# The vector engine's chained functions of an adaLN transformer kernel, divided at their joints and dealt among one another

## The reference

```python
mod = (silu(c) @ wmod).reshape(32, 6, 1, -1)          # sa, ca, ga, sb, cb, gb
ga = sign(ga) * max(|ga|, 0.25); gb the same
h = layernorm(x) * (1 + ca) + sa
x = x + ga * attention(h)        # rmsnorm, 16 heads of 64, causal softmax,
                                 # sigmoid gate per head, output projection
h = layernorm(x) * (1 + cb) + sb
x = x + gb * ffn(h)
# ffn: silu(h @ Wg + bg) * (h @ Wu + bu) @ Wd + bd, plus experts:
#   q = h @ Wq; sim with 64 keys for each of 4 heads and 2 halves
#   top 8 of each half, all sums of the two, the top 8 of those, softmax
#   sum over these 8 of 512 experts: silu(h . down[e]) * weight * up[e]
```

## Time and profile before

| | us |
|---|---|
| median of 3 runs | 1448.64 |
| lowest and highest | 1445.79, 1448.77 |
| span of the profiled execution | 1448.7 |
| PE busy | 1399.7 (97%) |
| DVE busy | 1289.4 (89%) |
| ACT busy | 1270.9 (88%) |
| POOL busy | 1052.9 (73%) |

### The profile page before, as it was taken

How to read it: one execution, slowest core, us unless ns; L and a number is a source line. 1 busy time by engine, 2 the same in 40 slices (tenths; PEclk the granted TensorE clock), 3 DMA queues, 4 the chain that set the end, 5 groups by cost and what they waited for, 6 DMA issues and landing times.

```text
span 1448.7 us, 39838 instructions
## 1 busy us (share of the span) xinstructions
PE 1399.7 (97%) x11491; PEld 1161.5 (80%) x11491; DVE 1289.4 (89%) x5345; ACT 1270.9 (88%) x4212; POOL 1052.9 (73%) x1221
## 2 busy tenths in 40 slices
PE   6899999999999999999999999999999999999998
PEld 4678788888788888788888788888788888788887
DVE  5589999999999999999999999999999999999977
ACT  6788988898988898988898988898988898988885
POOL 2048787778787777787777787787787777777760
PEclk9999999999999999999999999999999999999999
DMA  4000000000000000000000000000000000000000
GB/s 132 16 14 21 15 10 20 20 16 20 13 11 20 20 16 20 14 10 20 20 16 20 13 11 20 20 16 20 15 9 20 20 16 20 14 10 24 10 14 10
DMA packets 51041, 27.74 MB, mean 19 GB/s; under 512 B 10336, under 2 KB 50208, under 8 KB 51008
## 3 DMA queue, kind: packets, MB, share of 16 engines
q1 hardware_dynamic: 50768, 26.91, 7.1%
q10 hardware_dynamic: 240, 0.43, 0.1%
HBM read 23.02 MB, written 4.31 MB: 19 GB/s over the span
## 4 chain that ended last, share of the span: by engine, by line
PE 81%; ACT 14%; issue 3%; DVE 1%; DMA 0%; SPq 0%; POOL 0%; ACTq 0%; DVEq 0%; POOLq 0%
PE pW L1457 10%; PE pS L1527 9%; PE pW L1540 9%; PE pW L1568 8%; PE pW L1459 8%; PE pW L1458 8%; PE pS L1517 7%; PE pS L1513 6%; PE pW L1613 4%; PE pW L1610 4%; ACT pT L652 4%; ACT pS L660 4%; PE pW L1544 3%; PE pW L1601 2%; ACT h L750 2%
## 5 line engine op out<-in xcount | busy, mean ns | idle before, releaser
L660 ACT ACTIVATE pS<-pS,nmx 128x128 f32<-128x128 f32 (+1 forms) x1024 | 389.4, 433 | 33.2 <-DVE nmx L1085 33.2
L1085 DVE CUSTOM_DVE_ANT_0 pS<-pS,mask 128x128 f32<-128x128 f32 (+1 forms) x1024 | 331.8, 390 | 27.2 <-PE pS L1517 22.7
L504 POOL TENSOR_TENSOR fexp<-fexp,fsum 128x512 f32<-128x512 f32 x240 | 299.9, 1284 | 76.6 <-DVE fexp L1214 76.6
L652 ACT COPY pT<-pS 128x768 f32<-128x768 f32 x256 | 216.1, 844 | 42.2 <-PE pS L1527 40.4
L495 POOL TENSOR_TENSOR fsum<-ex 128x512 f32<-128x512 f32 x248 | 250.6, 1047 | 0.0
L1527 PE MATMUL pS<-ident,p_sb 128*128 128x128 f32 x1536 | 216.3, 277 | 6.1 <-DVE p_sb L1105 4.2
L1105 DVE TENSOR_TENSOR p_sb<-pS,coef 128x256 f32<-128x256 f32 (+2 forms) x512 | 210.5, 453 | 8.9
L1527 PEld LDWEIGHTS pS<-ident,p_sb 128*128 128x128 f32 x1536 | 173.7, 141 | 37.3 <-issue 18.9
L660 ACT ACTIVATION_READ_ACCUMULATOR pS<-pS,nmx 128x1 f32 x1024 | 193.7, 189 | 0.0
L642 ACT COPY qk<-pW 128x512 f32<-128x512 f32 x256 | 162.2, 634 | 4.6 <-PE pW L1459 1.1
L1540 PE MATMUL pW<-pT,v 128*64 128x256 f32 x1024 | 165.9, 402 | 0.3 <-ACT pT L652 0.2
(11 more groups left out here) (211 smaller groups left out, 3696.1 us busy)
## 6 DMA issues: line engine op xcount, KB each, us to landing
x_in<-in_L_attn_tokens SPq DMA_DIRECT2D x32, 128.0 KB, 2.1
x_res<-in_L_attn_tokens SPq DMA_DIRECT2D x32, 128.0 KB, 3.0
modB<-mods_dram SPq DMA_DIRECT2D x32, 128.0 KB, 2.9
modA<-mods_dram SPq DMA_DIRECT2D x31, 128.0 KB, 3.1
out<-yo SPq DMA_DIRECT2D x31, 128.0 KB, 1.9
modC<-mods_dram SPq DMA_DIRECT2D x32, 64.0 KB, 3.2
fsum<-in_L_attn_Wkv SPq DMA_DIRECT2D x1, 512.0 KB, 6.0
w_out<-in_L_attn_Wout SPq DMA_DIRECT2D x1, 512.0 KB, 7.2
```

The source lines that it names most:

```text
L504: ins = nc.gpsimd.tensor_tensor(fexp[:, k, h, :], fexp[:, k, h, :], fsum[:, k, h].rearrange("p i j -> p (i j)"), ALU.mult)
L652: nc.scalar.copy(pT[:, p % 2], pS[:, p % 2, :, 0:SW]).then_inc(S(pT_ready), 1)
L660: ins = nc.scalar.activation(ps, ps, ACT.Exp, bias=nmx[:, p % 2, h, k:k + 1], scale=-1.0, accum_out=den(p)[:, h, k:k + 1])
L1085: ins = nc.vector.tensor_tensor_reduce(out=ps, in0=ps, in1=mask[:, (1 - k) * P:2 * P], scale=-1.0, scalar=LARGEST, op0=ALU.add, op1=ALU.mi ...
```

## The change

The block functions of DVE are divided where `link` stood. The first part only increments the semaphore; the wait stands at the head of the next part. `normalise` becomes `invert`, `coefficients`, `normalise`; `ln1_stats` becomes `stats1`, `aggregate1`; `ln1_modulate` becomes `center1`, `scale1`, `shift1`, `square1`; `ln2_stats` becomes `gate_attention`, `add_residual`, `stats2`, `aggregate2`; `shift` becomes `row_largest`, `shift`, `shift_top`; `thresholds` becomes `top_candidates`, `sum_top`, `invert_top`; `finish` becomes `gate_output`, `finish`. The instructions and what they compute stay the same. In the loop's order the parts are dealt, so that another function's instruction stands between two dependent ones. The turns 0 and 32 call the parts one behind the other, in the old order. The orders of the other engines are as before.

```diff
-                def normalise(p):
+                def invert(p):
+                    if w.live(0):
+                        dve.wait_ge(S(exp_ready), at(exp_ready, i, p + 1))
+                        nc.vector.reciprocal(den(p), den(p)).then_inc(S(inverse_ready), 1)
+
+                def coefficients(p):
                     if w.live(0):
                         if p == 0:
                             w.wait_released("V", 0)
                             w.wait_released("V", NV)
-                        dve.wait_ge(S(exp_ready), at(exp_ready, i, p + 1))
-                        link(nc.vector.reciprocal(den(p), den(p)), attn_chain, i)
+                        dve.wait_ge(S(inverse_ready), at(inverse_ready, i, p + 1))
                         ins = nc.vector.scalar_tensor_tensor(out=coef[:, p % 2], ...
                         ins.then_inc(S(coef_ready), 1)
+
+                def normalise(p):
+                    if w.live(0):
                         dve.wait_ge(S(coef_ready), at(coef_ready, i, p + 1))
...
-                def ln2_stats():
+                def gate_attention():
                     if w.has("op"):
-                        dve.wait_ge(S(res_loaded), at(res_loaded, f, 16))
                         dve.wait_ge(S(modB_loaded), at(modB_loaded, f, 16))
                         w.wait_full("op")
                         o = w.bank("op")[:, 0:N].rearrange("p (k d) -> p k d", k=TB)
-                        link(nc.vector.tensor_tensor(o, o, modB[:, 0:1, :].broadcast_to([P, TB, D]), ALU.mult), head_chain, f)
+                        nc.vector.tensor_tensor(o, o, modB[:, 0:1, :].broadcast_to([P, TB, D]), ALU.mult).then_inc(S(head_chain), 1)
+
+                def add_residual():
...
+                def aggregate2():
+                    if w.has("op"):
+                        dve.wait_ge(S(head_chain), at(head_chain, f, 2))
                         apart()
                         for k in range(TB):
                             ins = nc.vector.bn_aggr(mv2[:, k, :], st2[:, k, :])
                         ins.then_inc(S(rstd2_in), 1)
...
-                thresholds()
+                top_candidates()
                 row_max(0)
+                sum_top()
+                invert_top()
                 choose(0, 0)
                 choose(0, 1)
                 row_max(1)
+                invert(0)
+                bias_product(1)
+                coefficients(0)
+                gate_product(1)
                 normalise(0)
-                bias_product(1)
-                gate_product(1)
+                invert(1)
+                gated_down(0)
+                coefficients(1)
                 normalise(1)
-                gated_down(0)
                 choose(1, 0)
                 gated_down(1)
                 row_max(2)
                 row_max(3)
                 bias_product(2)
+                invert(2)
+                gate_attention()
+                coefficients(2)
+                add_residual()
                 normalise(2)
-                ln2_stats()
                 gate_product(2)
+                stats2()
                 choose(1, 1)
+                aggregate2()
+                invert(3)
+                ln1(stats1)
+                coefficients(3)
+                ln1(aggregate1)
                 normalise(3)
-                ln1_stats()
                 bias_product(3)
                 gate_product(3)
                 row_max(4)
                 row_max(5)
                 low_part(h2T_high, h2T, "hT")
+                invert(4)
+                ln1(center1)
+                coefficients(4)
                 normalise(4)
+                row_largest(0)
+                invert(5)
                 shift(0)
+                coefficients(5)
+                ln1(scale1)
                 normalise(5)
-                ln1_modulate()
+                ln1(shift1)
+                row_largest(1)
+                ln1(square1)
                 shift(1)
+                shift_top()
                 row_max(6)
                 row_max(7)
+                invert(6)
                 low_part(xT_high, xT, "xT")
+                coefficients(6)
+                gate_output()
                 normalise(6)
+                invert(7)
                 finish()
+                coefficients(7)
                 bias_product(0)
                 normalise(7)
                 gate_product(0)
```

More of the change, by code:

```diff
@@ L1012, in _ @@
             stats1(0)
+            aggregate1(0)
             dve.wait_ge(load_nw, 16)
@@ L1017, in _ @@
             su_link(nc.vector.tensor_copy(cT[:, :], pW[0][:, 0:B]))
-            modulate1(0)
+            center1(0)
+            scale1(0)
+            shift1(0)
+            square1(0)
             def split_qkv(pieces):
@@ L1134, in low_part, with ln1 @@
                         w.release(nc.vector.tensor_tensor(parts[1][:, :], w.bank(name)[:, 0:N], parts[0][:, :], ALU.subtract), name)
[L1136 removed]
+                def ln1(part):
                     if w.live(1) and not first:
[L1138 to L1144 removed]
+                        part(i + 1)
+                def gate_attention():
                     if w.has("op"):
[L1146 removed]
                         dve.wait_ge(S(modB_loaded), at(modB_loaded, f, 16))
@@ L1162, in ln2_stats, with row_largest @@
                         ins.then_inc(S(rstd2_in), 1)
-                def shift(k):
+                def row_largest(k):
                     if w.has("sim", k):
@@ L1217, in choose, with gate_output @@
                             ins.then_inc(S(masks_ready), 1)
-                def finish():
+                def gate_output():
                     if w.has("y"):
@@ L1224, in finish @@
                         nc.vector.tensor_tensor(o, o, modC[:, 0:1, :].broadcast_to([P, TB, D]), ALU.mult).then_inc(S(y_gated), 1)
+                def finish():
+                    if w.has("y"):
                         dve.wait_ge(S(y_gated), at(y_gated, g, 1))
```

108 lines of the change are left out of this document (61 added, 47 removed).

## The result

The changed kernel takes 1587.39 us (median of 4 runs, 1586.56 to 1588.02), the kernel before 1448.32 (4 runs, 1445.79 to 1448.77). The ratio is 1.0961, with an interval of 1.0947 to 1.0974. Slower was forecast, but the 1587 lies 53 us above the 1534 of the forecast and 31 above the upper end of its range.

A forecast was written before the change was run, and what follows sets the result against it. PE, and for 7 us ACT, were taken to set the turn. Terms 0.8 + 1.2 + 0.55 + 0.3 = 2.85 us a turn, times 30 turns 85.5, on 1448.7 gave 1534 us; range 1475 to 1556.

The forecast's parts named there:

- What the dealing saves: 27 DVE joints get something between them, 0.11 us each: 3.0 us of DVE's time a turn, worth nothing beside PE's string.
- Pair 0: `bias_product(1)`, waiting for `u_sb`, stands ahead of `coefficients(0)` and `normalise(0)`; PE loses 0.8 us a turn, bounds 0 and 1.4.
- Pair 2 and the second layer norm: Gating ahead of `normalise(2)` and a late aggregation for POOL delay the scores of pair 5: 1.2 us, bounds 0 and 1.7.
- Pairs 4 and 5: `center1` and `scale1` ahead of `normalise(5)`, `square1` behind the maxima of `row_largest(1)`: 0.55 us a turn, bounds 0 and 0.9.
- Pair 6: `gate_output`, which needs "y", stands ahead of `normalise(6)`; PE loses 0.3 us a turn, bounds 0 and 0.5.
- Everything else: `invert(7)`, `finish`, `coefficients(7)` ahead of `bias_product(0)`, and the tail's maxima: costed at nothing.
- the bounds of 0 and 4.0: Bounds on the summed loss of 2.85 us a turn: 0 and about 4.0 (1.4 + 1.7 + 0.9).
- pair 1: `gated_down(0)`, needing ACT's tanh, ahead of `coefficients(1)`: 0.9 later for ACT, 0 us added, bounds 0 and 0.2.
- The rival B: Only part of the stalls: late aggregation alone (1509 us), or pairs 0 and 2 against PE (1473 us); chance 0.29.
- the wait for `u_sb`: Sign: in the profile after, DVE waits for `u_sb` in front of `coefficients(0)`, 0.8 us a turn, absent before.
- ACT's wait for `mr`: Sign: ACT waits for POOL's `mr` at `rows2` by 1 us or more, DVE's aggregation coming some 2 us later.
- the wait ahead of the gating: Sign: DVE waits for PE in front of the gating, 1 to 2 us a turn, absent before.

## Why the prediction was right or wrong

**What the dealing saves** was right in size and worth nothing, as said. DVE is busy for 39.41 us a turn, where it was 39.76. But that small difference hides more, for three instructions of the turn changed their neighbour on POOL: `center1` has grown by 1.94, `choose(1, 0)` by 0.76 (2.84 now, 2.08 before), and the difference of the tops in `shift_top`, which before ran beside POOL's product at 741.84, is 1.06 shorter (before, then after):

```profile
L1177 DVE TENSOR_TENSOR top_d<-top_s 128x128 f32<-128x128 f32 x31 | 39.5, 1274 | 0.0
```

```profile
L1203 DVE TENSOR_TENSOR top_d<-top_s 128x128 f32<-128x128 f32 x31 | 8.6, 278 | 0.0
```

With these taken out, the dealing saves 39.76 + 1.94 + 0.76 - 1.06 - 39.41 = 1.99 us of busy time. The prediction's 0.08 of overlap at 27 joints makes 2.16. The rest of its 3.0 is idle time: DVE's gaps of less than 0.12 us fall from 34 to 7 in a turn, 27 of them as counted, and by 1.18 us. What the prediction told of the Trainium skill, "VectorE: DVE Perf Modes", "The DRAIN you can't avoid", was half of it: the section also says that a next operation that is not held starts earlier, and that is what 0.94 against a length of 1.02 shows.

**Pair 0**: 0.8 predicted, 0.87 measured, and by the way that was named:

```profile
779.33 0.49 DVE L1132 SCALAR_TENSOR_TENSOR pW<-pW,b_g,u_sb 128x256 f32<-128x256 f32 x1 [0.94 <-ACT u_sb L698]
```

`bias_product(1)` waits for `u_sb` ahead of `coefficients(0)`, and PE stalls for 0.64 at the transposes. Putting the order back took that stall away, and 0.87 came back in each turn at full clock; in the others the clock took it again.

**Pair 2 and the second layer norm**: 1.2 predicted, 0.82 measured, and 0.90 in the run that put it back. The stall of PE at pair 2 came as worked out (0.5, 0.53). The aggregation starts 7.31 after `project_out` (793.35 less 786.04), where it was 5.62 after: 1.69 later against the 1.63 of the working (2.43 less 0.8). What was too dear is behind it:

```profile
793.35 0.24 DVE L1179 BATCH_NORM_AGGREGATE mv<-st 128x2 f32<-128x6 f32 x2
```

```profile
795.40 0.88 ACT L750 ACTIVATE h<-x,mr,rs 128x128 f32<-128x128 f32 x2 [0.44 <-POOL mr L551]
```

ACT's `rows2` comes 9.36 after `project_out`, before it was 8.43: 0.93 later, where the working says 1.17 (1.97 less 0.8). From the start of the aggregation to that of `mr` it is 1.82 us, and I had carried over the 2.12 of before. POOL's power for `rs` is shorter (after, then before), and so is the small step `nm` ahead of it, 232 ns in place of 368:

```profile
L549 POOL TENSOR_TENSOR rs<-ve,expo 128x2 f32<-128x2 f32 x32 | 22.9, 717 | 2.7
```

```profile
L549 POOL TENSOR_TENSOR rs<-ve,expo 128x2 f32<-128x2 f32 x32 | 27.1, 847 | 2.7
```

Before, `choose(1, 1)` of DVE lay beside it (726.04 to 727.04); in the changed kernel it is over by then. With this block put back in one piece, and `choose(1, 1)` behind it, the two means are 845 and 368 ns again. So the late aggregation was a little cheaper than its own lateness.

**Pairs 4 and 5: the step that failed.** 0.55 predicted, with an upper bound of 0.9, 2.51 measured. The mechanism was named, `center1` and `scale1` ahead of `normalise(5)`, but their price of 0.60 and 0.42 was read from rows in which POOL is idle, and the change puts `center1` where it is not. `center1` is released by POOL's `rs`, and the instruction that stands behind `rs` in POOL's queue is the first addition of `add_heads(1)`. So wherever DVE stands ready when `rs` comes, as it does here in each of the 27 turns (it waits 0.29, as worked out), the two start together, and `center1` takes 2.54 in place of 0.60. I had followed POOL's queue as far as `rs`, for the start time, and not looked at what comes behind it. That is one half of the error; the other is who stands behind `center1`. The 1.94 reach `normalise(4)` (PE 0.94), `coefficients(5)` and by it ACT:

```profile
758.99 0.73 ACT L667 ACTIVATE p_sb<-pS,coef 128x128 f32<-128x128 f32 x2 [2.38 <-DVE coef L1106]
```

and `shift(0)`, by it PE's second similarity, which takes the PSUM bank that `shift(0)` reads (PE 0.91). Of this last wait for a bank the prediction had no word. The run that put this block back returned 2.43 of the 2.51.

The Trainium skill has the rule that I should have weighed. "SBUF — State Buffer", in "SBUF: two separate sides", says that VectorE and GpSimd share a pair of ports that works as an exclusive lock: whichever of them starts first keeps it for its whole instruction, and the other is blocked. On VectorE's side it names instructions in a two-port mode and, against a GpSimd instruction that reads SBUF, as these additions do, those with two inputs in SBUF; and in "Who interferes with whom" it counts `tensor_scalar` among those that can enter such a mode. The traces agree: 0.34 to 1.22 for `center1`, a `tensor_scalar`, 0.42 to 1.30 for `scale1`, with two inputs in SBUF, and the 0.75 us between two starts of the masks against POOL's. They agree as well in what is not held up: `normalise(4)` reads its scores from PSUM, lies beside POOL's addition of 755.98, and takes the 1.02 of the earlier trace rows. In which mode an instruction runs no row shows.

**Pair 6**: 0.3 predicted, 0.29 measured by PE's positions; no run takes this dealing back alone. **Everything else**: nothing predicted, 0.05 measured. The growth of `choose(1, 0)` is not in it: the gating behind it still waited 0.52 for PE's projection.

So four of the five terms were good to 0.4, and the sum failed by 4.54 less 2.85, 1.7 us a turn; the bounds of 0 and 4.0 failed too, since the failing term's upper bound of 0.9 left POOL out as its value did. There is a slip in the 4.0 besides: it leaves out the upper bounds of pair 1 and pair 6, and with them, 1.4 + 0.2 + 1.7 + 0.9 + 0.5, it would be 4.7. That 4.54 lies below this is no merit of the working, for the term of 2.51 had an upper bound of 0.9. The rival B, only a part of the stalls, which held 0.29, was on the wrong side; the margins that I had doubted were as narrow as the rows showed. Of the signs that were named, the wait for `u_sb`, PE's waits at pairs 0 and 2 and the later aggregation are there; ACT's wait for `mr` is 0.44 and not 1, the wait ahead of the gating is 0.52 and not 1 to 2, and the turn is 48.0 and not 46.3.

## What to carry to other kernels

Before an instruction of VectorE is moved, look at what GpSimd runs at its new place, and take its duration from a row in which the same neighbour runs, not from the row of its old place; an instruction that stands waiting for GpSimd's result starts beside whatever GpSimd has next in its queue. Joints between dependent instructions are cheap (0.11 us here); what is dealt in between brings its own wait and everything that can stretch it to every result behind it in the queue. Where the waits of the bounding engine name another engine, as `pT` did here, the small gain lies with that engine's order: two swaps there gave 0.5%, all the dealing gave none.

## What the runs showed of the hardware that was not expected

- Side by side with GpSimd's work of 128x512, VectorE's 128x128 `tensor_scalar` took 1.22 us in place of 0.34, its 128x256 `tensor_tensor` from SBUF 1.30 in place of 0.42, its 128x128 `tensor_tensor` from SBUF 1.27 in place of 0.28, and two 128x512 `tensor_scalar` 2.19 or 2.94 in place of 1.00, the first with VectorE 0.45 us ahead, the second with it 0.02 behind.
- Taking such a meeting away by a wait moved it to the next instruction twice (0.34 and 1.30, then 0.42 and 1.15).
- After two stalls of TensorE of 0.94 and 0.91 us close to each other the granted clock fell to 0.50 for some 3 us in 18 of 29 turns of one kernel, at about 1 us each, and in two turns of another with the same two stalls. What else it took was not tested.
